# Four more query blocks pick their keys on TensorE, and the selection of the first tiles is packed ahead of block 10

## The reference, cut to what matters

```python
q_i = (x @ idx_wq).reshape(B_, L_, N_IDX_HEAD, D_HEAD)   # 4 index heads of 64
k_i = x @ idx_wk
s_i = relu(einsum('bthd,bsd->bths', q_i, k_i))
I = einsum('bths,h->bts', s_i, idx_w)
I = where(local, inf, I)                  # the last 64 keys are always in
I = where(causal, -inf, I)
_, idx = top_k(I, 96)                     # 64 local keys and 32 selected
key_c, value = (c_kv @ W_uk)[bi, idx], (c_kv @ W_uv)[bi, idx]
kr_sel = (x @ W_kr)[bi, idx]              # turned by the rank in idx
scores = (q_c . k_c + q_r . k_r) * scale
out = softmax(scores) @ v
```

## Time and profile before

| | us |
|---|---|
| median of 3 runs | 834.49 |
| lowest, highest | 827.72, 836.64 |
| the profiled execution's own time | 826.53 |
| its span | 824.6 |

### The profile page before, as it was taken

One profiled execution on the slowest core, in us unless ns is written; L12 is line 12 of the kernel. 1 busy time (PEld: TensorE's weight loads), 2 busy tenths in 40 slices (PEclk: granted clock), 3 DMA queues, 4 the chain that ended last, 5 costly groups with the idle time before them and its releaser, 6 DMA issues.

```text
span 824.6 us, 17320 instructions
## 1 busy us (share of the span) xinstructions
PE 770.4 (93%) x5725; PEld 460.6 (56%) x5725; DVE 648.0 (79%) x1906; ACT 508.7 (62%) x1461; POOL 507.6 (62%) x530
## 2 busy tenths in 40 slices
PE   8787899999999999999999999999999988999986
PEld 4334456565656565656566566566668444545543
DVE  4879798888999998979899999942232679696863
ACT  5556586675877878788787886686623334344230
POOL 6777777777777777777777777777710733211210
PEclk9898899999999999999999999999999999999999
DMA  8412211212111111111111111139136100000000
GB/s 275 93 26 54 53 36 42 50 36 41 31 28 31 25 32 30 26 31 30 27 31 27 30 29 27 31 87 227 49 116 179 52 0 1 1 13 2 13 6 22
DMA packets 58825, 39.97 MB, mean 48 GB/s; under 512 B 26961, under 2 KB 49713, under 8 KB 58545
## 3 DMA queue, kind: packets, MB, share of 16 engines
q1 hardware_dynamic: 41568, 21.57, 10.2%
q0 software_dynamic: 14336, 15.72, 9.5%
q10 hardware_dynamic: 2832, 1.58, 0.7%
HBM read 33.31 MB, written 5.55 MB: 47 GB/s over the span
## 4 chain that ended last, share of the span: by engine, by line
PE 58%; DVE 16%; ACT 9%; issue 8%; POOL 5%; DMA 2%; POOLq 0%; DVEq 0%; ACTq 0%; SPq 0%
PE psI L663 7%; PE psK L647 5%; ACT R L928 4%; PE psP L828 3%; PE psK L766 3%; PE psS L1771 3%; PE psS L802 3%; PE psP L835 3%; PE psK L754 3%; PE psP L817 2%; PE psS L805 2%; PE psP L647 2%; DVE SC L1144 2%; POOL R L1554 2%; PE psS L845 2%
## 5 line engine op out<-in xcount | busy, mean ns | idle before, releaser
L630 POOL DMA_INDIRECT G<-key_rows,idx x320 | 322.0, 1006 | 100.5 <-issue 95.2
L663 PE MATMUL psI<-kiT,qiT 64*128 64x512 f32 (+5 forms) x320 | 85.7, 559 | 13.6 <-ACT R L928 12.3
L647 PE MATMUL psK<-cst 128*128 128x512 bf16 x339 | 93.6, 383 | 1.3 <-ACT KT L1034 1.3
L1058 ACT ACTIVATE PT<-psP 128x256 f32<-128x256 f32 x128 | 48.4, 378 | 69.9 <-PE psP L835 64.5
L1144 DVE SCALAR_TENSOR_TENSOR SC<-R,w_x,SC 128x512 f32<-128x512 f32 (+5 forms) x120 | 78.5, 654 | 11.6 <-ACT R L928 8.5
L1172 DVE MAX8 top<-SC 128x8 f32<-128x128 f32 (+15 forms) x64 | 78.4, 1225 | 2.4
L1174 DVE FIND_INDEX8 idxf<-top,SC 128x8 uint32<-128x128 f32 (+15 forms) x64 | 78.3, 1223 | 0.0
L928 ACT ACTIVATE R<-psI 128x512 f32<-128x512 f32 (+5 forms) x160 | 73.3, 510 | 6.3 <-PE psI L663 4.8
L1562 POOL TENSOR_SCALAR rstd<-mv 128x4 f32<-128x4 f32 x13 | 3.6, 275 | 116.1 <-DVE mv L1978 116.1
L1026 ACT ACTIVATE PR<-PR,rinv 128x208 f32<-128x208 f32 x128 | 58.5, 457 | 26.2 <-DVE rinv L1335 25.6
L1034 ACT ACTIVATE KT<-psK 96x512 f32<-96x512 f32 x108 | 63.8, 591 | 15.6 <-PE psK L754 14.7
(11 more groups left out here) (352 smaller groups left out, 1725.0 us busy)
## 6 DMA issues: line engine op xcount, KB each, us to landing
G<-key_rows,idx POOLq DMA_INDIRECT x320, 2.5
rtmp<-idx_rows SPq DMA_DIRECT2D x20, 128.0 KB, 3.2
xslots<-zrow SPq DMA_DIRECT2D x4, 320.0 KB, 11.2
SC<-xslots SPq DMA_DIRECT2D x8, 160.0 KB, 2.5
yslots<-SC ACTq DMA_DIRECT2D x8, 160.0 KB, 2.4
V<-val_rows SPq DMA_DIRECT2D x15, 80.0 KB
xr<-in_x SPq DMA_DIRECT2D x1, 1024.0 KB, 11.7
qiT<-in_w_gate SPq DMA_DIRECT2D x4, 256.0 KB, 4.0
```

What stands on the lines that cost most here:

```text
L630: pool.indirect_dma_start(ring[o % RING][:, g % GPB, DR:], None, key_rows, bass.IndirectOffsetOnAxis(ap=idx[:, t, g:g + 1], axis=0),).then ...
L647: pe.matmul(ps[:, :].rearrange("p (a n) -> p a n", a=2), warm_w, warm_x, start=True, stop=True, skip_group_check=True)
L663: pe.matmul(psI[i][:, 0:w], lhs, kiT[64 * i:64 * i + 64, CH * c:CH * c + w], start=True, stop=True).then_inc(s["i_mm"], 1)
```

## The change

```diff
-HOT = (4, 5, 6, 7, 8, 9, 10, 11, 16, 17, 18, 19, 24, 25, 26, 27, 32, 33, 34, 35)
+HOT = (4, 5, 6, 7, 8, 9, 10, 11, 12, 13, 14, 15, 16, 17, 18, 19, 24, 25, 26, 27, 32, 33, 34, 35)
...
-START_ROOM = 1.1
+START_ROOM, LEAD, LEAD_LEVEL = 3.0, 5, 4.5
...
                 if n < 0:
                     left = min(left, 0.0) + START_ROOM
                 else:
-                    left = min(left, 0.0) + max(0.0, level - (0.7 if n >= 3 else 0.0) - other[n % NB] - hot(n))
+                    now = LEAD_LEVEL if item[1] - (item[0] == "sum") <= LEAD else level
+                    left = min(left, 0.0) + max(0.0, now - (0.7 if n >= 3 else 0.0) - other[n % NB] - hot(n))
```

## The result

| | before | changed |
|---|---|---|
| median of 17 runs each, us | 830.70 | 845.46 |
| lowest, highest | 826.91, 836.64 | 838.01, 856.79 |
| the profiled execution's own time | 826.53 | 846.87 |
| its span | 824.6 | 844.9 |

The change makes the kernel slower: the ratio is 1.0146, with a 95% interval of 1.0116 to 1.0176, so about 12 us. The executions of each kernel fall into two groups some 6 to 8 us apart (827 to 831 and 833 to 837 us before; 838 to 840 and 843 to 849 us, with two slower ones that the ratio leaves out, for the changed kernel), and the profile of before is of the faster group, that of the changed kernel of the slower. So the two profiled executions lie 20.3 us apart where the ratio says 12.

A forecast was written before the change was run, and what follows sets the result against it. It took TensorE to bound the kernel from step 10 on, VectorE in steps 2 to 9, GpSimd nearly. Terms 7.8 - 3.9 + 2.4 - 3.6 + 4.4 = +7.1 us on 834.5 gave 841.6 us, range 827 to 852.

The forecast's parts named there:

- the likeliest class, within 1%: Whole kernel: a time within 1% of before, chance 0.46, against 0.42 for slower and 0.12 for faster.
- rival A: Start: the packed selection brings one more low-clock stretch on TensorE; sum +14.8 us, median 849.3, chance 0.18.
- step 2 at 68 to 71 us: Sign that the forecast is right: step 2 begins at 68 to 71 us instead of 61.84.
- step 10 at 101 to 104: Sign that the forecast is right: step 10 begins at 101 to 104 us; before, it began at 94.69.
- Term 1: Ahead of step 1: 11.6 us more selection on VectorE, less 3.85 us of wait as cover; +7.8 us.
- Rival A's price: Cost of one low-clock stretch at the start: step 11's 8.33 us less the next step's 4.48, 3.85 us.
- Steps 2 to 9, said to stay: Steps 2 to 9: VectorE stays full with as much selection as before, so they cannot give term 1's time back.
- Terms 2, 3 and 4: Index pairs moved into TensorE's early gaps, -3.9 us; blocks 12 to 15, +2.4; TensorE's gaps from step 10, -3.6.
- Term 5: Loop's end: tile 14 is selected a step later, with 81.3 us of gathers behind it unchanged; +4.4 us.
- the ring being far ahead of use: GpSimd's gathers: a start some 10 us later costs nothing, as the ring of slots is far ahead there.
- Rival C: TensorE's gaps: packed work fills VectorE's 7.6 us of gaps, TensorE loses its 10.7; -8.2 us, median 826.3, chance 0.18.
- Rival B: Loop's end: tile 14 is selected in time, the tail hangs on TensorE alone; +2.7 us, median 837.2, chance 0.18.

The follow-up runs named there:

- e4: The changed kernel with the first queries' minimum, products, rotation and softplus issued ahead of the packed selection; ratio 1.0118 to the kernel before.
- e10: The changed kernel with 26 zero products filling TensorE's 5.9 us wait ahead of the first pair of sum 4.1; ratio 1.0128 to the kernel before.
- e3: The changed kernel with the selection's plan ending one step earlier (112), tile 14 selected at step 101; ratio 1.0072 to the kernel before.
- e5: The changed kernel with 34 slots for gathered keys instead of 28; ratio 1.0153 to the kernel before.
- e6: The changed kernel with the selection ending at step 112 (tile 14 at step 101) and 34 slots for gathered keys; ratio 1.0104 to the kernel before.
- e8: The changed kernel with three more fillers on TensorE ahead of the keys of blocks 124, 125 and 127; ratio 1.0176 to the kernel before.
- e2: The changed kernel with the old HOT list, so the packed plan without the change to blocks 12 to 15; ratio 1.0076 to the kernel before.
- e11: Kernel before with blocks 12 to 15 by 0/1 products, 34 gather slots, plan end 110, 0.7 us less selection a step in steps 1 to 9; ratio 0.9947.
- e7: Kernel before with blocks 12 to 15 by 0/1 products, 34 gather slots, INDEX_END 112, 1.2 us less selection a step in steps 1 to 9; ratio 1.0015.
- e1: The kernel before with only blocks 12 to 15 added to HOT and the old selection plan; ratio 0.9981 to the kernel before.
- e9: The changed kernel with 2.0 us of selection a step ahead of step 0 instead of 3.0; ratio 1.0104 to the kernel before.

## Why the prediction was right and wrong

It said 841.6 us, range 827 to 852, and forecast +7.1. The median is 845.5, and the ratio says +12.1. The sign and the range hold; the likeliest class, within 1%, does not: it is slower by 1.5%. The result lies nearer to rival A's +14.8 than to the forecast. That the forecast is off by 5 us only is in part luck: the start was 4.9 us short, two things that the sum puts at nothing, steps 2 to 9 and the end, cost 8.9 us between the two profiles, and by these profiles the whole is +20.3, of which the timed runs bear out 12. Of its signs, step 2 at 68 to 71 us and step 10 at 101 to 104 were missed (74.57 and 110.5), and GpSimd's saved time went mostly to tile 2 and to slots of the ring, with 0.87 us at tile 5 and none at tiles 3 and 8. By the steps:

- **Term 1, the packed selection, +7.8: mis-sized, measured +12.7 at step 2 and +11.7 to 12.9 in S over the five kernels with this start.** The work was right: VectorE is busy 11.7 us more in the first window (11.6 said), and `q_min` is 10.3 us later (10 said). The cover was wrong. I took the 3.85 us wait as gained, since its sum moved five steps forward; the relus of the sums moved with it are late again, and VectorE is idle 8.6 us in that window instead of 7.6. Two links in ScalarE's list make them late, the queries, which the prediction had, and the second score buffer, which waits for tile 2's selection and which it had not (e4). e10 parts the rest: with TensorE's clock held, S is 35.1, of it 2.2 us of cover found after all (idle 3.80 against before's 5.97); the slow clock takes 1.8 to 3.0 and undoes it. That is rival A's mechanism inside the forecast, at less than the 3.85 us that I had priced.
- **Rival A's price was misread.** It is the length of step 11 less that of step 12, but these steps differ in work, 58 matmul instructions and 49. TensorE is busy for the whole of step 11. At 0.73 of the clock its 8.33 us can lose 8.33 x 0.27 = 2.2 us at most, and these rows show no more than that. A's sign came true: between 23 us and the end of the loop the changed kernel has two stretches at low clock more than before, at 43.6 and 596.5 us. By the measured start, +12.7, the result stands between the forecast's +7.8 and A's +15.5, nearer to A.
- **Steps 2 to 9, said to stay: +3.1,** and 5.6 to 5.7 in e3, e5, e6 and e8. VectorE works 2.0 us more there (33.58 against 31.55), and the clock is 0.83 instead of 0.90. The prediction had counted as much selection there as before.
- **Terms 2, 3 and 4, together -5.1: measured -6.5** in steps 10 to 102. Blocks 12 to 15 cost 3.0 us in steps 10 to 17 (2.4 said). The rest, pairs and gaps, gave 10.5 in e2, where 7.5 was said. "A third" of TensorE's gaps was a guess and too little, but the pairs and the gaps were not tried apart.
- **Term 5, the gathers, +4.4: measured +5.0** from step 103 to block 127, and at the places named: 3.80 us of waiting ahead of tile 14, the last gather 81.6 us behind that selection, and a wait of TensorE for block 127. Undoing it (e3) gives back 0.7%, and e6 0.4% with overlapping intervals. The size is right partly by luck. e2 has 4.3 of these 5.0 us with tile 14 in time and GpSimd held by the slot of block 64 alone. And part of it is work: TensorE has 17 matmul instructions more in these steps than before (833 and 816), which in e10, at full clock, is 1.8 us more of busy time. But "the ring being far ahead of use" was false. Block 64 needs the slot of block 36, whose sums come at step 43. Its first gather starts at 257.47 instead of 243.79, 13.7 us later, and the last gather ends 12.7 us later: the lateness of TensorE there went nearly one to one into some 331 us of gathers without a stop. The late start would have reached the last gather without tile 14 too. With both chains loosened (e6) the end stays where e3 has it.
- **The end, not in the sum at all: +5.8** in this profiled execution, and less on the median. In seven of the kernels profiled TensorE waits 0.91 us or more for gathered keys at the loop's end; in six of them the clock falls within 3 us and the tail is 241.8 to 244.5 us. In e10, with 1.16 us, it does not fall. There the tail is 240.1. In the seven with 0.33 us or less it does not fall there either, and the tail is 238.5 to 239.6. That a wait of this kind brings the fall is likely by this count; e8, meant to show it, failed to remove the wait.
- **Rival C** failed ahead of step 2, where it had the packed work fill 7.6 us of gaps: it filled none. **Rival B** is out, as TensorE did wait at the end.

By the profiles, then, most of the loss arises ahead of step 2. From step 2 to block 127's minimum the changed kernel takes 525.7 us and before 524.1: all that packing VectorE ahead gave back later, 6.5 us, was lost again in steps 2 to 9 and behind step 103. By the timed ratios the late start costs less than it looks. e3 starts as late and ends the selection one step of the plan earlier, and only 6 of the 12 us are left in it.

What stays open: why the four blocks cost 5.6 us on top of the packed plan and nothing alone, of which the profiles place 3.0, and 2.7 in the old plan too; which part of the recovery is the pairs'; how the 12 us are shared between the start and the end; and where e11 gains on the kernel before.

## What to carry to other kernels

Work may be moved to where an engine idles only if what it waits for is there by then: in this start-up of chains through four engines, VectorE's 7.6 us of gaps took in none of 11.6 us of packed work. Take work off the second-busiest engine in the steps where the busiest waits for it, and put it where that engine has room (e7 and e11 against e1); a saved resource (here GpSimd's 21 us) may pay for the slack that this needs. Look at the same stretch in several executions before calling a difference of 1 or 2 us a gain. Before calling a ring of buffers far ahead, look which earlier block frees the slot of the first one of the longest stretch without a stop, and before moving work between buffers look which earlier tile must be done for the buffer to be free.

## What the runs showed of the hardware

Stretches at half clock stood beside short waits and were longer than these: behind 1.57 us of waiting the granted clock was 0.50 for 10.2 us, beside 2.15 us (e9) 17.1 us were at low clock, and the clock fell within the wait of 5.90 us, for 10.2 us in all. With that wait filled by products that nobody reads (e10) it did not fall there. In e10 a wait of 1.16 us brought nothing, and neither did one of 1.18 us at 522.19 in the kernel before, while in e3 a fall of 10.2 us stood beside waits of 0.49 and 0.78 us. What decides it is not shown. Nor does low clock always cost much: from step 103 to block 127 e3 had 10.2 us of it and took 90.5 us, before had none and took 89.3.

Indirect gathers of 128 x 64 without a stop took 1.29 us each on GpSimd, 256 of them 331.5 us (e3).
